# A four-layer graph network on one core: two node stages, each a loop of seven steps over single tiles, written out over pairs of tiles

## The reference

```python
h = jnp.maximum(_layernorm(x, axis=-1), 0.0)
x = x + _L0_gnn_ref(h, ...)       # filter, summed by source
x = h + gcn(h)                    # second layer: h plus relu(sum of messages + b)
x = x + _L2_gnn_ref(h, ...)       # attention over edges
x = x + _L3_gnn_ref(h, ...)       # GINE: messages, sums, a two-layer network
```

## Time and profile before

| | us |
|---|---|
| median of 3 runs | 6041.05 (6038.72 to 6041.3) |
| profiled execution, its own time | 6046.61 |
| span of its trace | 6045.4 |
| second layer's node stage, first activation to the next stage's first ACT instruction | 1964.72 to 2005.53 |
| fourth layer's node stage, the same | 4879.13 to 4919.73 |

### The profile page before, as it was taken

How to read it: one execution, slowest core, us unless ns; L and a number is a source line. 1 busy time by engine, 2 the same in 40 slices (tenths; PEclk the granted TensorE clock), 3 DMA queues, 4 the chain that set the end, 5 groups by cost and what they waited for, 6 DMA issues and landing times. The chain is left out here.

```text
span 6045.4 us, 103159 instructions
## 1 busy us (share of the span) xinstructions
PE 3497.4 (58%) x21281; PEld 2674.7 (44%) x21282; DVE 3568.2 (59%) x8518; ACT 1911.0 (32%) x4442; POOL 3799.9 (63%) x3879
## 2 busy tenths in 40 slices
PE   7858888888698333333353444444236645565556
PEld 5646666666575233333342222222136533444334
DVE  9858888888698433333354555555564454444444
ACT  7725555555344100000022222222147721111112
POOL 0047777777673577777716777777335537777774
PEclk9959999999898555555665555555579977667878
DMA  3069999999563211212218999999757622222221
GB/s 92 3 171 281 278 283 276 280 282 277 166 155 90 59 52 52 52 52 52 52 47 271 292 287 292 289 289 289 157 143 204 179 70 58 58 58 58 58 58 53
DMA packets 937029, 939.39 MB, mean 155 GB/s; under 512 B 330232, under 2 KB 777930, under 8 KB 936842
## 3 DMA queue, kind: packets, MB, share of 16 engines
q1 hardware_dynamic: 770906, 549.05, 33.6%
q0 software_dynamic: 137776, 369.86, 19.1%
q10 hardware_dynamic: 28288, 19.84, 1.1%
HBM read 686.22 MB, written 252.06 MB: 155 GB/s over the span
## 5 line engine op out<-in xcount | busy, mean ns | idle before, releaser
L1595 POOL DMA_INDIRECT edges_kv<-kv,edges_idx x880 | 839.2, 954 | 409.7 <-issue 268.0
L963 POOL DMA_INDIRECT by_src<-edges_rows,edges_pos x832 | 901.2, 1083 | 266.0 <-issue 259.9
L2225 POOL DMA_INDIRECT sum_rows<-table,sum_idx x832 | 806.6, 969 | 348.5 <-issue 253.4
L1322 POOL DMA_INDIRECT sum_rows<-table,sum_idx x832 | 790.1, 950 | 363.8 <-issue 251.2
L1399 PE MATMUL sum_p_sum<-sum_hot,sum_rows 128*128 128x128 f32 x1664 | 387.8, 427 | 665.7 <-DMA sum_rows<-table,sum_idx 665.7
L1399 PEld LDWEIGHTS sum_p_sum<-sum_hot,sum_rows 128*128 128x128 f32 x1664 | 360.0, 328 | 693.6 <-issue 693.6
L2323 PE MATMUL sum_p_sum<-sum_hot,sum_msg 128*128 128x128 f32 x1664 | 368.4, 412 | 473.5 <-DVE a_acc L2284 467.4
L1694 DVE TENSOR_TENSOR edges_kv<-edges_kv,edges_p_e 128x512 f32<-128x512 f32 x440 | 282.8, 684 | 532.1 <-DMA edges_kv<-kv,edges_idx 514.9
L2323 PEld LDWEIGHTS sum_p_sum<-sum_hot,sum_msg 128*128 128x128 f32 x1664 | 342.9, 314 | 558.5 <-issue 558.5
L1378 DVE TENSOR_TENSOR a_acc<-a_acc,sum_p_sum 128x128 f32 x832 | 235.6, 283 | 549.3 <-PE sum_p_sum L1399 548.2
L735 PE MATMUL edges_p_attr<-k_wekv,edges_attr 128*128 128x256 f32 x1664 | 476.4, 436 | 107.7 <-ACT edges_rows L810 105.9
(11 more groups left out here) (380 smaller groups left out, 8063.9 us busy)
## 6 DMA issues: line engine op xcount, KB each, us to landing
edges_ekv<-by_src SPq DMA_DIRECT2D x110, 1024.0 KB
v<-edges_kv SPq DMA_DIRECT2D x110, 512.0 KB, 4.1
sum_vv<-v SPq DMA_DIRECT2D x110, 512.0 KB, 3.9
edges_attr<-in_attr128T SPq DMA_DIRECT2D x104, 512.0 KB
edges_near<-h_in SPq DMA_DIRECT2D x832, 48.0 KB
sum_rows<-by_src SPq DMA_DIRECT2D x110, 264.0 KB, 3.0
edges_src_b<-rel SPq DMA_DIRECT2D x110, 256.0 KB
edges_dst_b<-dst SPq DMA_DIRECT2D x104, 256.0 KB
```

Source lines behind the costliest of these rows:

```text
L963: nc.gpsimd.indirect_dma_start(Dr.by_src0, bass.IndirectOffsetOnAxis(pos[:, q, j:j + 1], 0), rows[:, q % 2, j, :], None).then_inc(scattere ...
L1322: nc.gpsimd.indirect_dma_start(rows[:, q, j, :], None, Dr.table, bass.IndirectOffsetOnAxis(idx[:, q, j:j + 1], 0)).then_inc(fetched[q], 16)
L1595: nc.gpsimd.indirect_dma_start(kv[:, q, j, :], None, Dr.kv, bass.IndirectOffsetOnAxis(idx[:, q, j:j + 1], 0)).then_inc(fetched[q], 16)
L2225: nc.gpsimd.indirect_dma_start(rows[:, q, j, :], None, Dr.table, bass.IndirectOffsetOnAxis(idx[:, q, j:j + 1], 0)).then_inc(fetched[q], 16)
```

## The change

Both stages are written out as seven steps in Python instead of a loop on the engines. `hs` and `dh` (or `tab`) get two halves, used by step i at i % 2, `p_t` is a pair of PSUM tiles of two banks each, and the stores count on two semaphores, one for each half. ACT's step i waits for step i - 2 instead of i - 1; so does PE's wait for the copy out of `p_t`, and DVE's wait for the stores. On DVE the copy (or scaling) out of `p_t` of step i - 1 comes behind step i's work on `hs`, and in the first of the two stages the multiplication into `dh` comes ahead of the addition to `x`, whose end now signals both.

```diff
@@ -1251,49 +1251,56 @@
 
 def nodes_before_gcn(nc, K, Dr, s):
 
-    hs, dh = s.sb("h", [P, R, D]), s.sb("dh", [P, R, D])
-    p_t = s.ps("p_t", [P, 1024])
-    h_ready, x_ready, dh_ready, turned, kept, stored, tick = (s.sem(n) for n in ("h", "x", "dh", "t", "kept", "stored", "tick"))
+    hs, dh = s.sb("h", [P, 2, R, D]), s.sb("dh", [P, 2, R, D])
+    p_t = [s.ps(f"p_t{h}", [P, 1024]) for h in range(2)]
+    h_ready, dh_ready, turned, kept, tick = (s.sem(n) for n in ("h", "dh", "t", "kept", "tick"))
+    stored = [s.sem("stored0"), s.sem("stored1")]
     with nc.Block() as block:
         @block.scalar
         def _(act):
-            with nc.scalar.Fori(0, NI) as i:
-                act.wait_ge(dh_ready, i + 1)
-                normed(nc, K, act, i, hs, tick).then_inc(h_ready, 1)
+            for i in range(NI):
+                if i > 1:
+                    act.wait_ge(dh_ready, i - 1)
+                normed(nc, K, act, i, hs[:, i % 2], tick).then_inc(h_ready, 1)
 
         @block.vector
         def _(dve):
-            dve.sem_inc(dh_ready, 1)
-            dve.sem_inc(kept, 1)
+            def keep(i):
+
+                dve.wait_ge(turned, i + 1)
+                nc.vector.tensor_copy(K.acc[:, in_step(i)], p_t[i % 2][:, 0:R * P]).then_inc(kept, 1)
+
             nc.vector.memset(K.acc[:, NR:], 0.0)
-            with nc.vector.Fori(0, NI) as i:
-                x = K.x[:, bass.ds(i * R, R), :]
+            for i in range(NI):
+                x, h = K.x[:, i * R:(i + 1) * R, :], hs[:, i % 2]
                 dve.wait_ge(h_ready, i + 1)
-                nc.vector.tensor_tensor(out=x, in0=x, in1=hs[:], op=ALU.add)
-                dve.wait_ge(stored, i * 16 + 16)
-                dve.wait_ge(kept, i + 1)
-                nc.vector.tensor_tensor(out=dh[:], in0=hs[:], in1=K.dinv[:, bass.ds(i * R, R)].unsqueeze(2).broadcast_to([P, R, D]), op=ALU.mult).then_inc(dh_ready, 1)
-                dve.wait_ge(turned, i + 1)
-                dve.sem_inc(tick, 1)
-                nc.vector.tensor_copy(K.acc[:, in_step(i)], p_t[:, 0:R * P]).then_inc(kept, 1)
+                if i > 1:
+                    dve.wait_ge(stored[i % 2], 16 * (i // 2))
+                    dve.wait_ge(turned, i - 1)
+                nc.vector.tensor_tensor(out=dh[:, i % 2], in0=h, in1=K.dinv[:, i * R:(i + 1) * R].unsqueeze(2).broadcast_to([P, R, D]), op=ALU.mult)
+                nc.vector.tensor_tensor(out=x, in0=x, in1=h, op=ALU.add).then_inc(dh_ready, 1)
+                if i:
+                    keep(i - 1)
+            keep(NI - 1)
 
         @block.tensor
         def _(pe):
-            with nc.tensor.Fori(0, NI) as i:
-                pe.wait_ge(dh_ready, i + 2)
-                pe.wait_ge(kept, i + 1)
+            for i in range(NI):
+                pe.wait_ge(dh_ready, i + 1)
+                if i > 1:
+                    pe.wait_ge(kept, i - 1)
                 for r in range(R):
-                    tr = nc.tensor.transpose(p_t[:, r * P:(r + 1) * P], dh[:, r, :], K.ident[:])
+                    tr = nc.tensor.transpose(p_t[i % 2][:, r * P:(r + 1) * P], dh[:, i % 2, r, :], K.ident[:])
                 tr.then_inc(turned, 1)
 
         @block.sync
         def _(sp):
-            sp.sem_inc(stored, 16)
-            with nc.sync.Fori(0, NI) as i:
-                sp.wait_ge(dh_ready, i + 2)
-                sp.sem_inc(tick, 1)
-                nc.sync.dma_start(Dr.table.rearrange("(b p) d -> p b d", p=P)[:, bass.ds(i * R, R), :], dh[:]).then_inc(stored, 16)
-            sp.wait_ge(stored, 16 * NI + 16)
+            table = Dr.table.rearrange("(b p) d -> p b d", p=P)
+            for i in range(NI):
+                sp.wait_ge(dh_ready, i + 1)
+                nc.sync.dma_start(table[:, i * R:(i + 1) * R, :], dh[:, i % 2]).then_inc(stored[i % 2], 16)
+            for h in range(2):
+                sp.wait_ge(stored[h], 16 * ((NI + 1 - h) // 2))
 
 
 def sum_by_target(nc, K, Dr, s):
@@ -2109,23 +2116,25 @@
 def nodes_before_gine(nc, K, Dr, s):
 
 
-    hs, tab = s.sb("h", [P, R, D]), s.sb("tab", [P, R, D])
+    hs, tab = s.sb("h", [P, 2, R, D]), s.sb("tab", [P, 2, R, D])
     wc = s.sb("wc", [16, D])
     we1T, bc, bias, own = s.sb("we1T", [P, 2, 16]), s.sb("bc", [1, D]), s.sb("bias", [P, D]), s.sb("own", [P, 1])
-    p_t, p_w, p_c = s.ps("p_t", [P, 1024]), s.ps("p_w", [P, 512]), s.ps("p_c", [P, 4, P])
-    h_ready, tab_ready, turned, kept, stored, tick, w_ready, c_ready, blank, placed = (
-        s.sem(n) for n in ("h", "tab", "t", "kept", "stored", "tick", "w", "c", "blank", "placed"))
+    p_w, p_c = s.ps("p_w", [P, 512]), s.ps("p_c", [P, 4, P])
+    p_t = [s.ps(f"p_t{h}", [P, 1024]) for h in range(2)]
+    h_ready, tab_ready, turned, kept, tick, w_ready, c_ready, blank, placed = (
+        s.sem(n) for n in ("h", "tab", "t", "kept", "tick", "w", "c", "blank", "placed"))
+    stored = [s.sem("stored0"), s.sem("stored1")]
     with nc.Block() as block:
         @block.scalar
         def _(act):
-            with nc.scalar.Fori(0, NI) as i:
-                act.wait_ge(tab_ready, i + 1)
-                act.wait_ge(turned, i + 1)
-                normed(nc, K, act, i, hs, tick).then_inc(h_ready, 1)
+            for i in range(NI):
+                if i > 1:
+                    act.wait_ge(tab_ready, i - 1)
+                    act.wait_ge(turned, i - 1)
+                normed(nc, K, act, i, hs[:, i % 2], tick).then_inc(h_ready, 1)
 
         @block.tensor
         def _(pe):
-            pe.sem_inc(turned, 1)
...
-            with nc.tensor.Fori(0, NI) as i:
+            for i in range(NI):
                 pe.wait_ge(h_ready, i + 1)
-                pe.wait_ge(kept, i + 1)
+                if i > 1:
+                    pe.wait_ge(kept, i - 1)
                 for r in range(R):
-                    tr = nc.tensor.transpose(p_t[:, r * P:(r + 1) * P], hs[:, r, :], K.ident[:])
+                    tr = nc.tensor.transpose(p_t[i % 2][:, r * P:(r + 1) * P], hs[:, i % 2, r, :], K.ident[:])
                 tr.then_inc(turned, 1)
 
         @block.vector
         def _(dve):
-            dve.sem_inc(tab_ready, 1)
-            dve.sem_inc(kept, 1)
+            def keep(i):
+
+                dve.wait_ge(turned, i + 1)
+                nc.vector.tensor_scalar(K.acc[:, in_step(i)], p_t[i % 2][:, 0:R * P], own[:, 0:1], None, ALU.mult).then_inc(kept, 1)
+
...
-            with nc.vector.Fori(0, NI) as i:
+            for i in range(NI):
                 dve.wait_ge(h_ready, i + 1)
-                dve.wait_ge(stored, i * 16 + 16)
-                nc.vector.tensor_tensor(out=tab[:], in0=hs[:], in1=bias[:].unsqueeze(1).broadcast_to([P, R, D]), op=ALU.add).then_inc(tab_ready, 1)
-                dve.wait_ge(turned, i + 2)
-                nc.vector.tensor_scalar(K.acc[:, in_step(i)], p_t[:, 0:R * P], own[:, 0:1], None, ALU.mult).then_inc(kept, 1)
+                if i > 1:
+                    dve.wait_ge(stored[i % 2], 16 * (i // 2))
+                nc.vector.tensor_tensor(out=tab[:, i % 2], in0=hs[:, i % 2], in1=bias[:].unsqueeze(1).broadcast_to([P, R, D]), op=ALU.add).then_inc(tab_ready, 1)
+                if i:
+                    keep(i - 1)
+            keep(NI - 1)
 
         @block.sync
         def _(sp):
-            sp.sem_inc(stored, 16)
             sp.wait_ge(blank, 1)
             sp.wait_ge(c_ready, 2)
             for j in range(G):
                 nc.sync.dma_start(K.wc_g[16 * j:16 * (j + 1), j, :], wc[:]).then_inc(placed, 16)
-            with nc.sync.Fori(0, NI) as i:
-                sp.wait_ge(tab_ready, i + 2)
-                sp.sem_inc(tick, 1)
-                nc.sync.dma_start(Dr.table.rearrange("(b p) d -> p b d", p=P)[:, bass.ds(i * R, R), :], tab[:]).then_inc(stored, 16)
-            sp.wait_ge(stored, 16 * NI + 16)
+            table = Dr.table.rearrange("(b p) d -> p b d", p=P)
+            for i in range(NI):
+                sp.wait_ge(tab_ready, i + 1)
+                nc.sync.dma_start(table[:, i * R:(i + 1) * R, :], tab[:, i % 2]).then_inc(stored[i % 2], 16)
+            for h in range(2):
+                sp.wait_ge(stored[h], 16 * ((NI + 1 - h) // 2))
             sp.wait_ge(placed, 16 * G)
 
 
```

## The result

| | before | after |
|---|---|---|
| median of 6 runs each, us | 6040.28 (6035.44 to 6043.26) | 6001.26 (5998.09 to 6005.48) |
| ratio of the two, 95% interval | | 0.9938 [0.9927, 0.9949] |
| profiled execution, its own time | 6046.61 | 5998.09 |
| second layer's node stage, square root to the next stage's first ACT instruction | 42.83 | 27.70 |
| fourth layer's, the same | 42.34 | 27.58 |

The changed kernel is 39.0 us faster by the medians, 37.4 by the ratio (31 to 44 by its interval). The ratio, applied to the median of 6041.05 us that the forecast started from, gives 6003.6, just inside it.

The account below looks back on a forecast made before the run. Both node stages were taken as bound by the order of work, not by any engine. Savings of 14.9 us each, 29.7 together, off the 6041.05 us median gave 6011.3 us, range 6002 to 6021.

Parts of the forecast that it names:

- Sum of the stages: Second and fourth layers' node stages: each 14.86 us shorter, 29.7 us together.
- Entry: Start of both node stages: square root to first activation takes 1.34 us, instead of 2.02 and 1.74.
- Period of the second: Second layer's stage: DVE leads with `dh`, `x` and the delayed copy, 3.05 us a step instead of 5.355.
- Fourth: Fourth layer's stage: third `tab` waits for the first store, then ACT leads at 2.69 us a step; 14.9 us less.
- Tail: End of both node stages: the old distances to the next stage's first ACT instruction stay, 3.64 and 3.62 us.
- Which leaves 0.065 us for the loop's end: Second layer's old step of 5.355 us: after DVE's rows and wait, only 0.065 us remains for the loop's end.
- By the rows it takes out nothing: PSUM pair in the node stages: by itself it saves nothing as long as the order of work runs through ACT.
- the ring: Old node stages: engines work in turn through single tiles, with periods of 5.355 us (second layer) and 4.90 us (fourth).
- keeps the delayed copy harmless: PSUM pair in the node stages: its only effect is that the copy delayed by a step does no harm.
- My estimate by that advice: Node stages: by the skill's bank rotation the pair alone would remove a 1.09 us copy per step, 7.6 us per stage.
- the rival that ends slower: Later loops, such as the second layer's sums: moved code reloads each pass, 3.0 us in 26 passes, 6089 us; chance 0.04.
- The other half of my reasoning: Against reloading of moved loops: the instruction-loading queue moved 39 packets in the whole run, far fewer than reloading would need.

Follow-up runs that it names:

- e1: Kernel before with only the second layer's node stage changed, the fourth layer's left as it was: 7284.43 us, ratio 0.9975 [0.9950, 0.9999].
- e2: Kernel before with only the fourth layer's node stage changed, the second layer's left as it was: 7292.63 us, ratio 0.9978 [0.9953, 1.0002].
- e3: Kernel before with both node stages written out as Python loops, keeping single tiles and the old order of work: 7280.49 us, ratio 0.9989 [0.9964, 1.0015].
- e6: Changed kernel with one PSUM tile instead of the pair, PE waiting for the previous step's copy: 6013.93 us (one run).
- e5: Kernel before with 40 small transposes (80 PE instructions) ahead of PE's loop in the second layer's stage: 6032.72 us against 6040.41, ratio 0.9987 [0.9977, 0.9996].
- e9: Kernel before with 10 small transposes (20 PE instructions) ahead of PE's loop in the second layer's stage: 7190.18 us against 7222.87, one run.
- e11: Kernel before with 60 small transposes (120 PE instructions) ahead of PE's loop in the second layer's stage: 7219.9 us against 7222.87, one run.
- e4: The changed kernel once more, unaltered, on the chip of another group of runs, against the kernel before: 7250.71 us, ratio 0.9943 [0.9918, 0.9967].
- e7: Changed kernel with one more DVE memset per step, 896 columns in the second layer's stage, 512 in the fourth's: 6008.18 us (one run).
- e8: Changed kernel with placements issued two by two behind fourth-layer stores, and second-layer `dh` signalling PE and SP itself: 5998.75 us, ratio to before 0.9931.
- e10: Kernel before with 20 small transposes (40 PE instructions) ahead of PE's loop in the second layer's stage: 7216.1 us against 7222.87, one run.

## Why the prediction was right in its part, and too small as a whole

**Sum of the stages: right.** Forecast 29.7 us, measured 29.9 (15.13 and 14.76 against 14.86 each). e1 and e2 show that each comes from its own edit.

**Its terms.** *Entry*, 1.34 us: 1.35 in the fourth layer's (4845.50 - 4844.15), but 1.66 in the second's (1958.73 - 1957.07). *Period of the second*, 3.05: it is 3.00, the copy costs as little as the other two. *Fourth*: the third `tab` was to start 13.26 us after the square root and did after 13.42. Two errors hide in it: the first store started after 10.07 us instead of 10.26, and `tab` followed it by 3.35 instead of 3.0. The prelude did not move with ACT's entry by 0.40 us either, but by 0.20 (the placements began 5.18 us after the square root before, 4.98 after). The fifth tile's activations were to start after 14.46, and did after 14.65; from there 2.69 us a step, as forecast. *Tail*, 3.64 and 3.62: 3.41 in both (1984.77 - 1981.36 and 4871.73 - 4868.32). Errors of 0.1 to 0.3 us, of both signs, so that the sum came out nearer than its terms; that part of the agreement is luck.

**"Which leaves 0.065 us for the loop's end": wrong.** I looked for the loop's cost at its branch only. e3 measures 0.31 us a step. It lay in the gaps between the rows, which I had counted as handing over. From `dh`'s end to the transposes 0.14 us before and 0.06 in e3, from their end to the copy 0.23 and 0.04, from the copy's start to `x` 1.15 and 1.11: 0.31 together. The tail is the same: SP's store came 0.26 us after `dh`'s end (1970.02 - 1969.76) and now comes 0.02 after `x`'s (1963.69 - 1963.67). It did no harm to the sum, since the new period was built from DVE's rows without such gaps.

**"By the rows it takes out nothing": wrong for the fourth layer's stage.** The rows of before could show only that PE never waited for the copy as long as the ring ran through ACT. The change itself moves the scaling behind the next `tab`, and there one PSUM tile costs 5.3 us (e6). The words "keeps the delayed copy harmless" were right, and that is a part of the gain. The Trainium skill ("Perfetto Trace Analysis", Optimizing Tensor Performance, Matmuls) advises to rotate independent matmul groups through different PSUM banks, without a size. My estimate by that advice was 7.6 us a stage for the pair alone, in the old order; no run has that. In the new order e6 measures 0.9 and 5.3.

**Code at another place: the right mechanism with the wrong sign.** In the rival that ends slower I asked what a later loop pays when its code moves, and priced a loss of 3.0 us a pass. What happened is that a loop of before already paid about 0.30 us in each of 26 passes, 7.7 us of PE's waits in all, and stopped paying; the stage got 6.5 us shorter. I had looked only for a loss, and only in the second layer's sums. e5 reproduces it without the change: the stage is 5.5 us shorter, and the medians differ by 7.7 us (2 to 14), which is the figure of the pauses by chance; e1, e3 and e9 to e11 agree by the stage, and e2, which moves no PE code ahead of it, keeps it. It could have been read in the trace of before: waits for "issue" at the same row, once for each pass behind the first. The other half of my reasoning was that the queue that loads instructions moved only 39 packets; it still does in the profile after, so that this row says nothing on such a pause. The Trainium skill ("Runtime: NRT & Kernel Launch", Instruction fetch mechanics) says that a taken branch whose target lies outside the current window waits for a fetch; a pause at the loop's start that comes and goes with the code's place fits that, but no run here shows a fetch.

**What is left.** By the medians 39.0 - 29.9 - 6.5 = 2.6 us, by the ratio 1.0, less than the interval can tell. The stage lengths are those of one profiled execution of each kernel, and these two lie 48.5 us apart. Of the 12.1 us beyond the stages and the weighted sums, 3.0, 2.5 and 0.8 lie in the sums and the edge stage listed above, and 2.8 ahead of the first layer's square root. There, in the set-up, 28 matmuls took 6.21 us before and 3.89 after, and DVE's wait for them 7.1 and 4.8. The rows of the granted clock divide the kernels in that place: it stays at 1.00 (2.4 GHz) up to 290 us in the seven whose matmuls took 6.21 us (before, e1, e2, e3, e5, e6, e9), and from 278 us on it is 0.50 (1.2 GHz) in the six where they took 3.33 to 4.08 (after, e4, e7, e8, e10, e11). In both, PE had run these matmuls back to back at 1.00 until then. e4, e7, e8, e10 and e11 reach the first layer's square root 2.7 to 3.2 us sooner than before, as after does, although the clock is the lower one there. Neither the change, nor PE's code, nor the chip divides these two lists; why is open.

## What to carry to other kernels

When one tile of each kind is passed around between engines, write down every branch of the ring. Branches of the same length must all be doubled at once, and an operation that is delayed by a step makes the buffer that it frees matter. Read the waits for "issue" for a number of times that goes with a loop's passes: such a pause may vanish, or appear, when anything on that engine's list ahead of it changes its length, so a small gain or loss beside an edit should be tested with an idle edit of the same length. Look for a loop's address and semaphore work in the gaps between rows, too: here most of its cost lay there, not at the branch.

## What the runs showed of the hardware

PE's loop in the weighted sums stood still for about 0.30 us at each pass in one placement of its code (before and e2: 26 waits, 7.7 us) and in none of the others tried (shifts of 20, 40, 80 and 120 instructions, and those of the change and of e3), at a granted clock of 1.00 in all of them. Moving PE's code by 120 instructions went together with one slow issue on SP in another stage, 1.78 us instead of 0.59, in a single profile; whether it hangs on the place is open. The kernel before took 6040 us on one chip and 7307 on another. In the changed kernel's two traces (after and e4) the second layer's sums took 1050.9 and 1231.6 us, edge stage and softmax of the third 1257.1 and 1696.7, while the median gather instruction on POOL in those sums took 944 ns in both. Eight issues of small transfers one behind the other took SP 5.04 us; with the stores issued among them the stage was 1.7 us shorter (e8).
